# Softplus as one ScalarE function, six front products moved from GpSimd to VectorE, and new step sequences, in an RWKV-7 block

## Chip, cores and metric

The kernel runs on one core of one Trainium2 chip. The metric is device time in microseconds. A core has TensorE (PE), which multiplies matrices, VectorE (DVE), ScalarE (ACT), GpSimd (POOL) and SyncE (SP), which here issues DMAs. Each engine runs its own instructions in order. They are tied together by semaphores alone.

## The reference

For x of shape (2, 4096, 256) the block computes, with a layer norm xn in front:

```
xx  = previous token of xn - xn
mix = tanh((xn + xx*maa_x) @ w1) @ w2                 (four parts)
xrg, xwa, xk, xv = xn + xx * (maa_. + mix_.)
r, k, v = xrg @ wr.T, xk @ wk.T, xv @ wv.T
w   = -softplus(-(time_decay + tanh(xwa @ d1) @ d2)) - 0.5
g   = tanh(xrg @ g1) @ g2
kk  = normalised per head (k + tanh(xk @ kkk1) @ kkk2)
a, ma, mk = sigmoid(aaaaa + xwa@..), sigmoid(misc_a + xwa@..), sigmoid(misc_k + xk@..)
k   = k*ma + k*a*(1-ma);   k = k * exp(min(w*mk, 0))
S_t = S_{t-1}*diag(exp(w_t)) + (S_{t-1} (-kk)) (kk*a)^T + v_t k_t^T ;  y_t = S_t r_t
y   = (group norm(y)*ln_w + ln_b + bonus) * g @ wo.T
out = x + y * silu(ffn(xn))                           (ffn: gated, hidden 768)
```

All of it is float32, with 4 heads of 64 in each of the 2 sequences.

## The kernel before

The 4096 tokens are cut into 16 tiles t of 256 tokens; a tile covers both sequences, so it has 512 columns. In a tile the recurrence is worked in 8 chunks of 32 tokens, each chunk in 4 blocks of 8. A big product over a tile has the shape 128x1024 (two halves of the 256 channels by 512 columns), half of it 128x512.

The program is a software pipeline of sections. In a section, four tiles are in work at once: `norm` of tile i+1, the front of tile i (`mixing`, `decays`, `key`, `receptance`, `value`, `update`, `pairs`), the recurrence `back` and the `ffn` of tile i-1, and `output` of tile i-2. Each of these stages is a Python generator for each engine, and each `yield` ends a step. What comes after what on an engine is written out by hand as a string of letters (`ORDER` for full sections, `FIRST` before there is a recurrence, `LAST` when there is no front): each letter takes the next step of its stream, in `walk`. The letters are L norm, F mixing, D decays, K key, R receptance, V value, E update, X pairs, N ffn, B back, O output.

The steps used below are these.

- On PE: `mixin`, `mix0`, `mix1` (L) make the four mix parts. `lora` and `z` (F) make the decay's logits and those of the sigmoids. `k0`, `k1`, `hk`, `kk`, `rn` (K), `gh`, `r0`, `r1` (R), `v0`, `v1`, `vT0`, `vT1`, `g0`, `g1` (V) are the projections. N steps are half groups of four matmuls of the feed-forward. `half`, `matrix`, `KT` 0 to 3 (X) make pairwise products and transposed keys. `band`, `corner` and, for each chunk c, `state`, `u`, `values`, `s`, `y` are the recurrence (B). `yT0`, `yT1`, `out0`, `out1` are the output.
- On ACT: `na`, `nma` are sigmoids, `z0`, `z1` hold the decay's first activations, `mk0`, `mk1` sigmoids, `sqk` squares for the key's norm, `rn_ln` and `rn` its inverse root by Ln and Exp, `em`, `er`, `ek`, `es`, `EF` exponentials.
- On DVE: `mix..` are the mix products (L989), `nd`, `cs2`, `cs4`, `cs8` and `fl3` to `fl0` the cumulated decay, `unit`, `inv0` to `inv14`, `flip` the inversion of the small triangular matrices, `kk0`, `kk1`, `rn0`, `rn1`, `k`, `b`, `rk`, `dm`, `qa`, `qa0`, `hat0`, `hat1` the front's products, `near`, `far`, `keys` the keys for PE.
- On POOL: the mix sums (L1273), for each chunk the faded state `state` (L1334), and the products `mixa`, `kk`, `mkz`, `kem`, `e3`, `qr`.

The decay is made in four parts. ACT takes Abs and Relu of z + decay (L718, L721). ACT then applies Exp and Ln(1 + .) to the whole tile (L850, L853), which gives softplus as relu(-x) + ln(1 + exp(-|x|)). DVE adds 0.5 (`n`, L999) and limits to 20 (`nd`, L1002).

PSUM is held as two rings. `ring` has four banks, `spare` four others, shared with the recurrence's chunk banks. Each use waits until the use four places before it has been emptied (`room`, `early_room`). `KT3` and the mix matmuls are neighbours in `ring`. The matmul helper `project` (L381) has many callers: `lora` and the projections.

SP issues the DMAs in order (`invert`). The matrices go out to DRAM and come back in another layout. The inverse's part leaves after DVE's `flip`, comes back as `first`, for which SP also waits for `out1` of PE, and only then can PE run `band`.

Of the kernel before, what the change touches and what calls it, by code (L numbers as in the profile page):

```python
# [1525 lines left out]
```

## Time and profile before

| | us |
|---|---|
| median of 3 runs | 1663.23 |
| lowest and highest | 1652.58, 1664.02 |
| profiled execution, its own time | 1652.18 |
| profiled execution, span from first to last instruction | 1650.7 |
| granted TensorE clock, mean (1 is 2.4 GHz) | 0.981 |

The profile is one execution, and its durations add up to its own span and not to the median. Engines overlap: their busy times are shares of the same span. Busy time counts an instruction from its start to its end. TensorE's matmuls overlap each other, so the step from one group's start to the next group's start is the cost of a group. L and a number is a line of the kernel, and a name with an arrow says what is written from what.

### The profile page before, as it was taken

How to read it: one execution, taken by the hardware profiler on the slowest of the kernel's cores; microseconds unless marked ns; L12 is line 12 of the kernel's file. 1: busy time of each engine (PE TensorE's matmuls, PEld its weight loads, DVE VectorE, ACT ScalarE, POOL GpSimd, SP SyncE). 2: the span in 40 equal slices, each digit the busy share in tenths (PEclk: the TensorE clock that was granted, in tenths of full speed). 3: DMA queues.
4: the chain of work that ended last, by engine and by line, in shares of the span. 5: the costliest groups of instructions: out<-in, count | busy, mean ns of one | idle time of the engine just before them, and what ended most of it. 6: DMA issues, size and time to landing. Idle time of an engine off the chain costs nothing.

```text
span 1650.7 us, 48315 instructions
## 1 busy us (share of the span) xinstructions
PE 1543.8 (94%) x20288; PEld 1084.1 (66%) x20288; DVE 1157.5 (70%) x2581; ACT 1126.8 (68%) x1954; POOL 579.1 (35%) x459
## 2 busy tenths in 40 slices
PE   4599999999999999999999999999999999999887
PEld 1266667576676757667676766757667675766665
DVE  3776768778676877867678676767767687686633
ACT  4858586676858767685876858667585876768412
POOL 3424432433433244343423433243343323434101
PEclk9789999999999999999999999999999999999989
DMA  4011110201112021111202111020111202111020
GB/s 145 14 19 34 32 33 16 60 19 32 34 33 46 16 47 31 32 33 26 53 16 42 36 33 33 17 59 19 32 34 27 52 16 47 31 33 33 11 55 27
DMA packets 251431, 57.86 MB, mean 35 GB/s; under 512 B 223696, under 2 KB 250704, under 8 KB 251088
## 3 DMA queue, kind: packets, MB, share of 16 engines
q1 hardware_dynamic: 241936, 41.95, 13.5%
q10 hardware_dynamic: 9280, 12.81, 2.2%
q8 instruction: 162, 2.65, 0.7%
q14 instruction: 53, 0.43, 0.1%
HBM read 36.38 MB, written 18.35 MB: 33 GB/s over the span
## 4 chain that ended last, share of the span: by engine, by line
PE 88%; DVE 4%; ACT 3%; POOL 2%; issue 2%; DMA 1%; SPq 0%; ACTq 0%; DVEq 0%; POOLq 0%
PE bank L535 22%; PE chunk L381 15%; PE bank L545 10%; PE bank L510 8%; PE bank L665 4%; PE chunk L643 3%; PE chunk L615 3%; PE chunk L590 3%; POOL big L1273 2%; PE bank L480 2%; PE chunk L629 2%; PE bank L381 2%; PE bank L486 2%; PE chunk L599 2%; PE bank L518 1%
## 5 line engine op out<-in xcount | busy, mean ns | idle before, releaser
L1334 POOL TENSOR_TENSOR SF<-ST,CT 128x256 f32<-128x256 f32 x128 | 101.9, 796 | 302.1 <-DVE ST L1200 302.1
L535 PE MATMUL bank<-xT,wu 128*128 128x256 f32 x768 | 203.3, 396 | 0.0
L535 PE MATMUL bank<-xT,wg 128*128 128x256 f32 x768 | 198.2, 390 | 0.0
L545 PE MATMUL bank<-wd,hT 128*128 128x256 f32 x768 | 179.5, 388 | 1.9 <-DVE hT L1160 1.9
L535 PEld LDWEIGHTS bank<-xT,wg 128*128 128x128 f32 x768 | 141.5, 191 | 49.6 <-issue 30.3
L545 PEld LDWEIGHTS bank<-wd,hT 128*128 128x128 f32 x768 | 144.1, 193 | 23.3 <-DVE hT L1160 3.0
L535 PEld LDWEIGHTS bank<-xT,wu 128*128 128x128 f32 x768 | 135.4, 189 | 33.0 <-issue 9.9
L381 PE MATMUL chunk<-KS,W 128*128 128x512 f32 x320 | 148.8, 603 | 1.5 <-POOL KS L1273 1.5
L510 PE MATMUL bank<-qpad,KS 128*64 128x32 f32 x4096 | 144.1, 226 | 5.6 <-DVE KE L1132 4.0
L510 PEld LDWEIGHTS bank<-qpad,KS 128*64 128x64 f32 x4096 | 132.0, 141 | 17.4 <-issue 8.7
L381 PE MATMUL chunk<-big,W 128*112 128x512 f32 (+1 forms) x256 | 125.6, 614 | 16.9 <-POOL big L1273 16.9
L912 ACT ACTIVATE rhs<-chunk 96x256 f32<-96x256 f32 x128 | 48.7, 380 | 127.0 <-PE chunk L615 125.7
L895 ACT ACTIVATE Y<-chunk 32x256 f32<-32x256 f32 x256 | 96.3, 376 | 51.2 <-PE chunk L599 47.9
L869 ACT ACTIVATE sg<-bank 128x512 f32<-128x512 f32 x96 | 57.0, 594 | 100.9 <-PE bank L535 94.3
L1283 POOL MEMSET KS<- 128x800 f32 x16 | 12.2, 765 | 291.0 <-PE chunk L381 291.0
L381 PEld LDWEIGHTS chunk<-KS,W 128*128 128x128 f32 x320 | 59.8, 191 | 70.7 <-issue 66.8
L844 ACT ACTIVATE KT<-bank 128x512 f32<-128x512 f32 x64 | 38.2, 597 | 95.4 <-PE bank L518 94.7
L1195 DVE COPY VU<-chunk 32x256 f32<-32x256 f32 x128 | 53.4, 417 | 66.7 <-PE chunk L629 63.5
L1160 DVE TENSOR_TENSOR hT<-sg,bank 128x512 f32<-128x512 f32 x96 | 65.7, 684 | 45.2 <-PE bank L535 33.1
L1273 POOL TENSOR_TENSOR big<-VU,xT 128x512 f32<-128x512 f32 x64 | 74.3, 1197 | 58.2 <-DVE VU L989 58.2
L832 ACT ACTIVATE qpad<-big 64x256 f32<-64x256 f32 x256 | 91.6, 405 | 1.2
L1273 POOL TENSOR_TENSOR KS<-VU,xT 128x512 f32<-128x512 f32 x64 | 91.2, 1459 | 0.0
(161 smaller groups left out, 3484.8 us busy)
## 6 DMA issues: line engine op xcount, KB each, us to landing
smalls<-in_x SPq DMA_DIRECT2D x32, 256.0 KB, 3.1
Y<-in_x SPq DMA_DIRECT2D x32, 256.0 KB, 3.1
out<-fsil ACTq DMA_DIRECT2D x32, 256.0 KB, 2.5
scrA<-AM SPq DMA_DIRECT2D x64, 64.0 KB, 1.9
hat<-scrB SPq DMA_DIRECT2D x32, 128.0 KB, 3.1
hat<-scrF SPq DMA_DIRECT2D x32, 128.0 KB, 3.1
KE<-scrA SPq DMA_DIRECT2D x64, 32.0 KB, 2.2
scrT<-KE SPq DMA_DIRECT2D x16, 128.0 KB, 1.7
```

What stands on the lines that cost most here:

```text
L381: m = pe.matmul(o, weights[:, h, :], x[:, h, :], start=(h == 0), stop=(h == NH - 1))
L510: q = pe.matmul(oc[:, :, BL * j:BL * j + BL], K[:, 2 * n + b, 64 * j:64 * j + 64], Q[:, 2 * n + b, j, :, :, :].rearrange("p a b e -> p (a ...
L535: q = pe.matmul(o[:, TT_ * n2:TT_ * n2 + TT_], w[:, h, 128 * (n + n2):128 * (n + n2) + 128], x_now[:, h], start=(h == 0), stop=(h == NH - 1))
L545: q = pe.matmul(o[:, 256 * m:256 * m + 256], hT[:, n, 128 * m:128 * m + 128], wd[:, n, :], start=(n == 0), stop=(n == NF - 1))
L665: q = pe.matmul(o[:, 256 * n2:256 * n2 + 256], yb[:, h, 128 * m:128 * m + 128], wo[:, h, :], start=(h == 0), stop=(h == NH - 1))
L832: i = act.activation(Q[p0:p0 + 64, :, :, hh, x, :], own[p0:p0 + 64, qs], ACT.Copy)
L869: act.activation(sg[:, :], ring.tile(key)[:, :], ACT.Silu).then_inc(*sg_ready.up)
L895: i = act.activation(by_batch, RY[64 * x + 32:64 * x + 64, :, :].rearrange("p b (g n) -> p b g n", g=NH), ACT.Copy)
L1160: i = dve.tensor_tensor(hT[:, n:n + 2, :], sg[:, :].rearrange("p (n c) -> p n c", n=2), ring.tile(key)[:, :].rearrange("p (n c) -> p n c", ...
L1195: dve.tensor_copy(VU[par][32:64, c, :].rearrange("p (g x n) -> p x g n", g=NH, x=2), PU[32:64, :, :].rearrange("p x (g n) -> p x g n", g=N ...
L1273: pool.tensor_tensor(columns(dst[:, h, :]), columns(w[:, h, :]), x_now_of(par, h), ALU.add).then_inc(*moved.up)
L1334: pool.tensor_tensor(SF[:, :, :, :], ST[:, :, :, :], fade[:, c].unsqueeze(3).to_broadcast([128, B, NH, N]), ALU.mult).then_inc(*faded.up)
```

## The change

It does three things. `Softplus` of ACT takes the place of Abs, Relu, Exp and Ln, and DVE's `n` and `nd` become one instruction. The six POOL products `mixa`, `kk`, `mkz`, `kem`, `e3`, `qr` become DVE instructions of the same shape (scalar_tensor_tensor). All strings of `ORDER` and `FIRST` are new; `LAST` stays.

```diff
-ORDER = {"pe": ("FNNKOOFNNOKNOVNNNKNNVKRRRKBNNBVNNNNBBNBBNBNBNBBVBBEBNVBBNBBVBBBNBBNBXBBXBBNXBNBBXBBXBBBLBBNXBXBBXBBN"
-            "LXXXLLX"),
-         "act": ("NFKFFFFFFDDVKNKNVKKRKEOOBRKBVKRXDXXBVBNNBNBBVVBXBBXBVBBBBBVBNBBLBBXBLLXBBBXBBXNXLX"),
-         "dve": ("OBOOBBBNBBBBBOBBOBBDBDBNDBBDKDDKKDKNEDDXEEBXBNXBXBXEXXXBEXBNXXBXXBLXBBXXXXBLXXBXNBXXXXXBXXXBLLXXXBBX"
-             "XLLLLLLLL"),
-         "pool": ("DBEXEFKXBBBBLLBBBBLLLLLLLL")}
+ORDER = {"pe": ("NNNFNKOOFNNORVNNNNKKOVKRBNKBNRNNVBBNBBNBNBNBBVNNBBEBVBBNBBVBNBBNBBXBXBBNXBBNBNBBXBBXBXBBNBBLBNBBXXBB"
+            "LXXXXLL"),
+         "act": ("NFKFFFFFRFVNKKNVOKKKBEBOKRKRDXXBXBVNBVNBBVVNBBBXBVVBBXBBBBNBBXXBLBBLXLBXBBNBBLXX"),
+         "dve": ("ONBOOBBBBBDBBBBBBBNBBDBBDDOOKKDXEFKKNDEDEXDKEEBXBXXXNBXBXXXBEXXBEXXBXNBXLBXXXBXXBLXBXNXXXBXXXBXLXLBX"
+             "XXBBXXLLLLLLLL"),
+         "pool": ("DBBBBBBLBBLBLLLLLLLL")}
...
-                            act.activation(az[:, g, :], spare.tile(key), ACT.Abs, bias=v("decay", g))
...
-                            act.activation(rz[:, g, :], spare.tile(key), ACT.Relu, bias=nv("decay", g), scale=-1.0).then_inc(*z_ready.up)
+                            act.activation(rz[:, g, :], spare.tile(key), ACT.Softplus, bias=nv("decay", g), scale=-1.0).then_inc(*z_ready.up)
...
-                act.wait_ge(*z_ready(t))
-                act.activation(az[:, :, :], az[:, :, :], ACT.Exp, scale=-1.0).then_inc(*dz_exp.up)
-                yield "exp"
-                act.wait_ge(*dz_exp(t))
-                act.activation(az[:, :, :], az[:, :, :], ACT.Ln, bias=one[:, 0:1]).then_inc(*dz_ln.up)
-                yield "ln"
...
-                dve.wait_ge(*dz_ln(t))
-                dve.scalar_tensor_tensor(out=rz[:, :, :], in0=az[:, :, :], scalar=0.5, in1=rz[:, :, :], op0=ALU.add, op1=ALU.add).then_inc(*n_ready.up)
-                yield "n"
-                dve.wait_ge(*n_ready(t))
-                dve.tensor_scalar(nd[:, :, :], rz[:, :, :], MAXDECAY, None, ALU.min).then_inc(*nd_ready.up)
+                dve.wait_ge(*z_ready(t))
+                dve.tensor_scalar(nd[:, :, :], rz[:, :, :], 0.5, MAXDECAY, ALU.add, ALU.min).then_inc(*nd_ready.up)
...
+                dve.wait_ge(*rn_ready(t))
+                dve.scalar_tensor_tensor(out=kk[:, :, :], in0=kk[:, :, :], scalar=1.0, in1=rn[:, :, :], op0=ALU.mult, op1=ALU.mult).then_inc(*kk_ready.up)
+                yield "kk"
...
-                pool.wait_ge(*rn_ready(t))
-                pool.tensor_tensor(kk[:, :, :], kk[:, :, :], rn[:, :, :], ALU.mult).then_inc(*kk_ready.up)
-                yield "kk"
...
```

The other five products change engine in the same way as `kk`. On PE the end of a full section was

```
... y7 ffn1 mixin KT2 half3 matrix3 mix0 mix1 KT3 | lora gate00 gate01 k0 yT0 yT1 z up00 up01 out0 k1 ... kk gh r0 r1 rn band
```

and is now

```
... y7 mixin KT2 half3 matrix3 KT3 mix0 mix1 | gate00 gate01 up00 lora up01 k0 yT0 yT1 z gate02 gate03 out0 gh v0 up02 up03 gate04 gate05 k1 hk out1 v1 kk r0 band up04 rn corner up05 r1
```

On DVE the front of a full section is now: groupnorm, up00, unit, yT0, yT1, inv0 to inv4, nd, inv5 to inv11, up02, inv12, inv13, cs2, inv14, flip, cs4, cs8, out0, out1, kk0, kk1, fl3, e3, mkz, mixa, rn0, rn1, up04, fl2, kem, fl1, k, dm, fl0, kk, b, rk, u0, qa, s0, qa0, qr, hat0. On ACT it is: gate00, lora, k0, na0, nma0, z0, z1, na1, gh, nma1, v0, gate02, k1, hk, gate04, v1, out0, mk0, mk1, sqk, band, em, corner, out1, rn_ln, r0, rn, r1, EF, er, ek, state0, es, u0, vT00, ffn0, state1.

## Rows read from the trace of the kernel before

**Rows 1.** The page, part 1: busy us, share of the span, instructions.
```profile
PE 1543.8 (94%) x20288; PEld 1084.1 (66%) x20288; DVE 1157.5 (70%) x2581; ACT 1126.8 (68%) x1954; POOL 579.1 (35%) x459
```

**Rows 2.** Windows: length, busy per engine, then granted PE clock, DMA share, GB/s.
```profile
0.00:34.40 34.40, 11.62 (x36) 4.77 (x36) 12.93 (x27) 10.93 (x14) 12.33 (x21) 1.00 0.49 174
34.40:109.60 75.20, 51.97 (x404) 30.66 (x404) 54.94 (x98) 51.28 (x80) 30.66 (x21) 0.80 0.06 13
301.20:398.50 97.30, 94.56 (x1272) 66.86 (x1272) 71.89 (x162) 70.21 (x123) 36.01 (x29) 1.00 0.17 34
985.00:1084.00 99.00, 96.25 (x1268) 67.44 (x1269) 70.89 (x161) 70.03 (x123) 36.00 (x28) 0.98 0.16 33
1475.70:1650.70 175.00, 154.68 (x2112) 115.28 (x2112) 91.43 (x212) 82.38 (x154) 33.55 (x28) 0.94 0.15 33
976.00:980.00 4.00, 3.63 (x6) 1.73 (x7) 3.50 (x5) 0.01 (x1) 4.00 (x5) 0.62 0.45 45
805.00:826.00 21.00, 21.00 (x145) 13.90 (x144) 8.12 (x16) 18.33 (x25) 12.61 (x7) 1.00 0.34 64
```

**Rows 3.** Waits of PE: who waited for whom, us in total, times, longest.
```profile
PE chunk L381 <- POOL big L1273: 16.9, 16, 2.6
...
PE bank L518 <- DVE VU L989: 12.1, 14, 0.9
PE bank L495 <- DVE KS L1057: 9.5, 1, 9.5
...
PE chunk L421 <- issue: 5.4, 13, 0.5
...
PE bank L510 <- DVE KE L1132: 4.0, 1, 4.0
```

**Rows 4.** Timeline of PE: start, length, instruction, count, idle before it and releaser.
```profile
679.13 1.14 PE L402 MATMUL chunk<-smalls,W 32*128 32x512 f32 x8
...
682.13 0.66 PE L518 MATMUL bank<-con,KE 128*128 128x128 f32 x4 [0.87 <-DVE VU L989]
683.77 1.94 PE L381 MATMUL chunk<-big,W 128*112 128x512 f32 x4 [0.98 <-POOL big L1273]
...
690.42 0.70 PE L421 MATMUL chunk<-smalls,W 32*128 32x512 f32 x2 [0.39 <-issue]
```

**Rows 5.** Timeline of PE, the same place three periods on.
```profile
976.37 3.18 PE L381 MATMUL chunk<-big,W 128*112 128x512 f32 x4 [0.99 <-POOL big L1273]
```

**Rows 6.** Groups by line and form, ACT: busy us, mean ns, idle before.
```profile
L718 ACT ACTIVATE big<-chunk,vec 128x512 f32<-128x512 f32 x32 | 22.0, 689 | 0.0
...
L850 ACT ACT_TABLE_LOAD x16 | 20.5, 1283 | 0.3
...
L853 ACT ACTIVATE big<-big,one 128x1024 f32<-128x1024 f32 x16 | 18.4, 1149 | 0.2
...
L850 ACT ACTIVATE big<-big 128x1024 f32<-128x1024 f32 x16 | 16.9, 1057 | 0.2
```

**Rows 7.** Groups by line and form, POOL.
```profile
L1278 POOL TENSOR_TENSOR big<-KB,big 128x1024 f32<-128x1024 f32 x16 | 38.1, 2380 | 1.5 <-ACT big L712 1.5
```

**Rows 8.** Groups by line and form, DVE.
```profile
L1227 DVE SCALAR_TENSOR_TENSOR hat<-hat,vec,gT 128x512 f32<-128x512 f32 x32 | 32.3, 1010 | 1.1
...
L1049 DVE SCALAR_TENSOR_TENSOR KB<-KB,KS 128x1024 f32<-128x1024 f32 x16 | 19.6, 1225 | 36.6 <-POOL KS L1288 36.6
...
L1055 DVE SCALAR_TENSOR_TENSOR KS<-KS,vec,KB 128x512 f32<-128x512 f32 x16 | 11.9, 746 | 0.7 <-issue 0.7
```

**Rows 9.** The page, part 6: a DMA, KB, us from issue to landing.
```profile
hat<-scrF SPq DMA_DIRECT2D x32, 128.0 KB, 3.1
```

**Rows 10.** Timeline of ACT: sqk, first half and second half.
```profile
811.44 0.63 ACT L745 ACTIVATE KS<-KS 128x512 f32<-128x512 f32 x1 [0.22 <-DVE KS L1027]
812.09 1.28 ACT L747 ACTIVATE KS<-KS 64x512 f32<-64x512 f32 x2
```

**Rows 11.** Timeline of PE between the end of kk and rn.
```profile
808.52 5.42 PE L381 MATMUL chunk<-KS,W 128*128 128x512 f32 x12
```

More of the change, by code:

```diff
@@ L135, in program @@
         mask = sb("mask", [128, 64], U32)
-        one = sb("one", [128, 2])
-        minus_half = one[:, 1:2]
+        minus_half = sb("minus_half", [128, 1])[:, 0:1]
         wg = sb("wg", [128, NH, DH])
@@ L993, in mixing @@
             def mixing(t):
-                yield from ()
+                dve.wait_ge(*nma_ready(t))
+                dve.scalar_tensor_tensor(out=mix_a[:, :, :], in0=na[:, :, :], scalar=1.0, in1=nma[:, :, :], op0=ALU.mult, op1=ALU.mult).then_inc(*mixa_ready.up)
+                yield "mixa"
             def decays(t):
                 rz = gT[t % 2]
-                dve.wait_ge(*dz_ln(t))
-                dve.scalar_tensor_tensor(out=rz[:, :, :], in0=az[:, :, :], scalar=0.5, in1=rz[:, :, :], op0=ALU.add, op1=ALU.add).then_inc(*n_ready.up)
-                yield "n"
-                dve.wait_ge(*n_ready(t))
-                dve.tensor_scalar(nd[:, :, :], rz[:, :, :], MAXDECAY, None, ALU.min).then_inc(*nd_ready.up)
+                dve.wait_ge(*z_ready(t))
+                dve.tensor_scalar(nd[:, :, :], rz[:, :, :], 0.5, MAXDECAY, ALU.add, ALU.min).then_inc(*nd_ready.up)
                 yield "nd"
@@ L1042, in update @@
                 par = t % 2
+                rz = gT[t % 2]
+                dve.wait_ge(*z_ready(t))
+                dve.wait_ge(*mk_ready(t))
+                dve.scalar_tensor_tensor(out=mk[:, :, :], in0=rz[:, :, :], scalar=0.5, in1=mk[:, :, :], op0=ALU.add, op1=ALU.mult).then_inc(*mkz_ready.up)
+                yield "mkz"
+                dve.wait_ge(*em_ready(t))
+                dve.wait_ge(*kk_raw(t))
+                dve.scalar_tensor_tensor(out=kT[:, :, :], in0=kT[:, :, :], scalar=1.0, in1=mk[:, :, :], op0=ALU.mult, op1=ALU.mult).then_inc(*kem_ready.up)
+                yield "kem"
                 dve.wait_ge(*mixa_ready(t))
@@ L1070, in pairs @@
                 dve.wait_ge(*cs_ready(t))
+                dve.wait_ge(*mixed(t))
+                dve.scalar_tensor_tensor(out=e3b, in0=csb[:, :, BL - 1:BL].to_broadcast([128, G8, BL]), scalar=1.0, in1=csb,
+                                         op0=ALU.mult, op1=ALU.subtract).then_inc(*e3_raw.up)
+                yield "e3"
                 dve.wait_ge(*kem_ready(t))
@@ L1082, in pairs @@
                 yield "qa0"
+                dve.wait_ge(*qa_most(t))
+                dve.wait_ge(*r_ready(t))
+                dve.scalar_tensor_tensor(out=qr[:, :, :], in0=er[:, :, :], scalar=1.0, in1=rT[:, :, :], op0=ALU.mult, op1=ALU.mult).then_inc(*qr_ready.up)
+                yield "qr"
                 dve.wait_ge(*qr_ready(t))
@@ L1276, in mixing @@
             def mixing(t):
-                pool.wait_ge(*nma_ready(t))
-                pool.tensor_tensor(mix_a[:, :, :], na[:, :, :], nma[:, :, :], ALU.mult).then_inc(*mixa_ready.up)
-                yield "mixa"
+                yield from ()
             def decays(t):
@@ L1286, in key @@
             def key(t):
-                pool.wait_ge(*rn_ready(t))
-                pool.tensor_tensor(kk[:, :, :], kk[:, :, :], rn[:, :, :], ALU.mult).then_inc(*kk_ready.up)
-                yield "kk"
+                yield from ()
             def receptance(t):
@@ L1297, in update @@
             def update(t):
[L1298 to L1317 removed]
+                yield from ()
+            def pairs(t):
+                yield from ()
             def ffn(t):
@@ L1344, in output @@
                 yield from ()
-            for level, col in ((1.0, 0), (-0.5, 1)):
-                pool.memset(one[:, col:col + 1], level).then_inc(s_clear, 1)
+            pool.memset(minus_half, -0.5).then_inc(s_clear, 1)
             for z in (xT2[1][:, :, :, TT_:TT_ + 1], ST[:, :, :, :], TT[:, :, :], qpad[0][:, :, :, :, :, :], qpad[1][:, :, :, :, :, :]):
```

34 lines of the change are left out of this document (8 added, 26 removed).

## Prediction

> **What bounds the kernel now.** I read the page first, its busy times by engine. TensorE (PE) is busy 1543.8 of the span's 1650.7 us [rows 1]. The diff touches none of its 20288 matmuls, so only the 107 us in which PE has no work can shrink, plus what a lower clock costs. The busy times by stretch show where they are [rows 2]: a steady period has 2.7 us without work in 97.3, the first front 23.2 in 75.2, the loads and first `norm` before it 22.8, and the tail from the last `z` 20.3 in 175, mostly in an order that the diff leaves alone. PE's waits name them [rows 3]. The timeline of one section boundary places them [rows 4]: `KT3` (L518) stands behind `mix1` and waits 0.87 us for a bank that VectorE's (DVE's) mix product L989 frees. `lora` (L381) then waits 0.98 us for the second mix sum of GpSimd (POOL, L1273), and `z` (L421) loses 0.39 us.
>
> The granted clock matters too. Periods of 99.0 us instead of 97.3 hold a stretch at 1.2 instead of 2.4 GHz [rows 2]. The clock falls right behind the KT3 and lora waits: the same four `lora` matmuls take 3.18 us instead of 1.94 [rows 4, 5]. The profiled execution has three such periods (the `lora` at about 976, 1075 and 1175 us), each 1.7 us longer.
>
> **The change, part by part.** I call the start of `mix0` on PE 0 and walk the new order with durations of before. From one group's start to the next is less than its printed length: an N half (L535, four matmuls) 0.87, a 128x512 projection (L381) 1.72 to 1.78 us, as the timeline's starts show.
>
> *The boundary.* The new PE order is matrix3, KT3, mix0, mix1, gate00, gate01, up00, lora, up01, k0, yT0, yT1, z. `KT3` is now ahead of the mix matmuls and needs nothing of L989: -0.87. Behind `mix1` (over at 2.0) come three N halves, so `lora` is reached at 4.6. Before, POOL's second sum let it start at 683.77 - 679.13 = 4.64 [rows 4], and on that way nothing changes, so of the 0.98 about 0.05 stays. `z` keeps its 0.4 (10.5 to 12.75).
>
> *Softplus.* Out per section: two Abs (0.69), Exp (1.06), Ln (1.15) and their two table loads (1.28) [rows 6]. Relu becomes Softplus. No row shows Softplus; its neighbours of this shape take 0.69, which I take, with 0.57 (their spacing) and 1.4 (Abs and Relu together) as bounds. Nor does a row show whether Softplus shares a table with Sigmoid. If it does, no load comes in; if not, one before `z0` and one before `na1` do. I take not, since here Exp and Ln too, common as they are, have a load each. ScalarE (ACT) then runs load, na0, nma0 (to 13.0), load, z0, z1 (15.6), load, na1, gh (18.6), nma1 (19.2). PE's `gh` at 16.2 needs z0 (15.0), `v0` at 17.9 needs z1: hidden. At 1.4 us each, `up02` on DVE and the inversion behind it slip by 1.4, and with a band load that has 0.7 to spare that is up to 10 us in all.
>
> By the row a table load is 1.28 us with at most 0.3 around it [rows 6]. The Trainium skill ("ScalarE: Activation LUTs", What ACT_TABLE_LOAD costs) budgets about 2.66 us for each switch, a drain included, and its section on table sets asks to batch by set, which a Softplus among Sigmoids does not. By its figure two loads out and two in cancel as well.
>
> *Products on DVE.* A POOL product of 128x1024 takes 2.38 us [rows 7], five of the six moved are like it; on DVE the shape takes 1.22 [rows 8]. DVE gains six and loses `n`: +6.1 a section, 98 us in all, to about 1255. POOL falls to about 360. The cover is DVE's own waiting: between 805 and 826 us it is busy 8.1 of 21 us [rows 2], part of the rest in waits for these very POOL products.
>
> Side by side the two engines may hinder each other: DVE's L1227 takes 1.01 us on mean, L1055 of the same shape 0.75 [rows 8], and L1227 runs while POOL's mix sums do. The Trainium skill ("SBUF — State Buffer", Who interferes with whom) says that a DVE instruction with two SBUF inputs contends with a GpSimd one that reads SBUF, which all six products are. The trace agrees so far. By that rule a state product (L1334) could stand behind one of them, 1.2 us. PE's next state update is further off than that, so I add nothing.
>
> *The front.* After `z` PE has gate02, gate03, out0 (from 14.5; its input is ready at 14.0 to 14.6: 0.1 lost), gh, v0, four N halves, k1, hk, out1, v1 (to 29.95), kk, r0, band, up04, and wants `rn` at 34.8. `rn` needs `sqk` from ACT, and ACT starts its part when v1 ends: v1 0.6, load 1.28, mk0 and mk1 1.26, sqk 1.93 [rows 6, 10] give 35.2. That is a **new wait of 0.5 us**; before, three projections (5.4 us) lay between kk and rn [rows 11]. DVE: inversion to 25.1, cs4, cs8, out0, out1, kk0, kk1 (32.5), fl3, e3, mkz (35.5), mixa, rn0, rn1 (37.9), up04, fl2, kem (40.3), k, dm (42.9), kk (behind ACT's rn, 43.7), b, rk (48.4), u0 (48.85). PE wants `s0` at 49.4: **0.5 us to spare**, and ACT's u0 (48.85, behind er, ek, es) has as much. PE's `u1` waits 0.15 for ACT's `state1`. From `half0` on DVE is 0.5 us or more ahead at each step. The band's load left SP 2.5 us after the flip by the timeline of SP and takes 3.1 us [rows 9]; now it also stands behind out1, and lands by 32.1. PE wants it at 32.8.
>
> Per period: -0.87 - 0.93 + 0.5 + 0.15 + 0.1 + 0.05 = -1.0, in 14 periods **-14 us**. The three clock falls behind the waits removed: 3 x 1.7 = **-5 us**.
>
> *First front and tail.* There PE waits in plain sequence, 9.5 us for rk and 4.0 for the keys besides others [rows 3]. `nd` can start about 5 us earlier, kk is 1.15 shorter; against it, ACT takes k0 ahead of lora (+1), and the next x and the vT copies stay. I get the first `half0` at 76 to 77 us instead of 80.6 and 3 to 4 us of this at the second `z`, which also has two N halves more behind it (1.7 us less in the tail): **-5 us**, bounds 0 and -12 (the 13.5 us of the two waits less what must stay).
>
> Sum: 1652.2 (the profiled execution's own time) - 14 - 5 - 5 = 1628. That execution lies 11 us under the median of before, 1663.2. Six more clock falls at the same boundary would explain it, but no row shows the other runs. With the boundary closed I expect the median near the profiled one and add 2: **1630 us**, 2% less.
>
> **The rivals.**
> - *New waits take the place* (0.20). rn, s0 and the band stand within 0.7 us of their data in my walk. If they lose 1.0 us a period more, the boundary's gain is given back: 1628 + 14 = 1642, with the clock falls back as well 1647, with the median's distance 1658. For it: ACT has no pause up to sqk. Against: inside a steady section PE had no wait longer than 0.4 us. This is most of "same".
> - *DVE becomes the bound of the front* (0.09), the slower side. Place: rk, then u0 on DVE, `s0` on PE. DVE has 7.3 us of products more ahead of u0. Each us beyond the 0.5 to spare costs 14; slower by over 1% needs a wait of 3.6 us a period at `s0`, a DVE that is 4.1 us later than in my walk. At 4.8 late it gives about 1690. Against: 12.9 us idle before in this stretch, 7.3 to place.
> - *Softplus shares Sigmoid's table and rn does not wait* (0.10). Two loads (2.57 us) less let gate02 and the inversion run ahead, and without the 0.5 and other small waits it is 1628 - 7 - 4 = 1617.
> - *Only the head gains; the boundary waits move but stay* (0.05): 1652 - 5 = 1647 profiled, median 1655 to 1658.
> - Forecast: 0.56.
>
> **How the numbers follow.** About 1%, 16.6 us, is what measurement tells from no change: faster is below 1646.6, slower above 1679.9. Faster: 0.56 + 0.10 + 0.04 of the first rival = 0.70. Slower: 0.09, with 0.01 for Softplus at 1.4 and a late band together = 0.10. Same: 0.20. The range goes from 1610, the third rival with a better head, to 1658, the top of the first and fourth; outside lie the slower rival and 0.1 of others. The likeliest case's own range is 1618 to 1643.
>
> **What would show each step.** PE's wait at the chunk L381 for POOL L1273 falls from 16.9 us to under 5, and L518's for L989 is gone; else the boundary is wrong. The period from L421 to L421 is 96.2 to 96.5; at 97 or more the first rival holds, and the line that waits names the step (L455 for ACT: sqk; L564 for DMA: band; L643 for DVE: the slower rival). Softplus rows are 0.69 us, table loads stay nine a section. DVE is busy about 1255 us, POOL 360. The first L510 starts at 76 to 77 us. No clock fall at the boundary in the steady part. The prediction falls if the products take clearly over 1.22 us on DVE, or if PE's own busy time grows.

## The result, and the profile after

| | before | after |
|---|---|---|
| median, us | 1663.62 (4 runs, 1652.58 to 1664.95) | 1605.62 (4 runs, 1604.55 to 1612.88) |
| ratio after to before | | 0.9675, 95% interval 0.9632 to 0.9717 |
| profiled execution, its own time | 1652.18 | 1604.90 |
| its span | 1650.7 | 1603.4 |
| granted TensorE clock, mean | 0.981 | 0.988 |

The change makes the kernel 58 us faster, 3.3%. The forecast was 1630, with a range from 1610 to 1658. The direction was right, but the time lies 4.4 us below the range, and the gain is 58 us where 33 were forecast. L numbers of after are its own lines, mostly one or two below those of before.

First the page of after, part 1, beside [rows 1]:

```profile
PE 1520.5 (95%) x20288; PEld 1064.9 (66%) x20288; DVE 1243.6 (78%) x2661; ACT 1069.5 (67%) x1889; POOL 354.6 (22%) x362
```

PE has the same 20288 matmuls and is busy 23 us less. The forecast had only the clock falls' 5 us of that. DVE (1255 forecast) and POOL (360) came out near what was worked out.

The windows of after, cut as [rows 2] (length, busy per engine, granted clock, DMA share, GB/s): first front, a steady period, tail.

```profile
35.50:103.60 68.10, 50.43 (x414) 30.84 (x415) 55.60 (x106) 46.67 (x75) 13.64 (x13) 0.82 0.10 19
386.70:481.80 95.10, 93.76 (x1268) 65.82 (x1268) 77.52 (x167) 66.60 (x119) 22.05 (x23) 1.00 0.17 34
1434.70:1603.40 168.70, 148.19 (x2104) 110.16 (x2104) 97.06 (x216) 79.02 (x150) 19.45 (x22) 0.96 0.16 34
```

A steady period, from `z` to `z`, takes 95.12 us. Before, an undisturbed one took 97.26. That splits into 1.39 us less idle (2.75 to 1.36) and 0.75 less busy (94.51 to 93.76). The first front is 7.1 us shorter, the tail 6.3.

PE's waits in after, beside [rows 3] (engine, line, releaser, us in total, times, longest):

```profile
PE bank L534 <- DVE VU L981: 13.5, 15, 1.0
PE bank L494 <- DVE KS L1060: 7.8, 1, 7.8
...
PE chunk L420 <- issue: 5.5, 14, 0.4
PE bank L509 <- DVE KE L1143: 4.0, 1, 4.0
...
PE chunk L380 <- POOL big L1284: 2.9, 2, 2.6
```

The wait of `lora` (L380) for POOL fell from 16.9 to 2.9 us. KT3's wait for the mix product is gone, but `gate00` (L534) now waits for the same product, 13.5 us in 15 waits. PE's timeline at the boundary shows it, beside [rows 4]:

```profile
469.94 0.66 PE L517 MATMUL bank<-con,KE 128*128 128x128 f32 x4
470.52 1.14 PE L401 MATMUL chunk<-smalls,W 32*128 32x512 f32 x8
471.49 1.04 PE L406 MATMUL bank<-smalls,W 32*128 32x512 f32 x8
473.42 2.00 PE L534 MATMUL bank<-xT,wg 128*128 128x256 f32 x8 [0.89 <-DVE VU L981]
475.25 1.03 PE L534 MATMUL bank<-xT,wu 128*128 128x256 f32 x4
476.12 1.88 PE L380 MATMUL chunk<-big,W 128*112 128x512 f32 x4
```

The ring is filled in turn. Whatever follows the four mix matmuls of the second half takes a bank that DVE has to empty first. Before, that was `KT3`; now it is `gate00`.

The operations themselves, from the groups by line and form of ACT and then of DVE (count, busy us, mean ns, idle before):

```profile
L719 ACT ACT_TABLE_LOAD x16 | 20.5, 1283 | 12.0 <-DVE hat L1238 11.9
...
L719 ACT ACTIVATE gT<-chunk,nvec 128x512 f32<-128x512 f32 x32 | 20.3, 684 | 0.2
```

```profile
L1092 DVE SCALAR_TENSOR_TENSOR big<-big,KS 128x1024 f32<-128x1024 f32 x16 | 26.0, 1625 | 0.0
...
L987 DVE SCALAR_TENSOR_TENSOR big<-KB,big 128x1024 f32<-128x1024 f32 x16 | 19.5, 1217 | 0.0
```

Softplus takes 0.68 us and has a table load of its own. Five of the six products take 1.22 us on DVE. `qr` (L1092) takes 1.63 on mean. It begins while POOL works on a state product (L1325), on POOL's and DVE's timelines:

```profile
426.85 0.71 POOL L1325 TENSOR_TENSOR SF<-ST,CT 128x256 f32<-128x256 f32 x1 [18.99 <-DVE ST L1211]
426.99 1.65 DVE L1092 SCALAR_TENSOR_TENSOR big<-big,KS 128x1024 f32<-128x1024 f32 x1
```

It ends 1.08 us after the state product, which is nearly its whole length of 1.22. The experiments come back to this.

### The profile page after: what moved, and what is told of

It is laid out like the page before. It is cut to its first block, busy times and chain, and to the rows that moved or that the text cites. A ratio compares the mean times of both kernels' runs of the same rounds, so it can differ in the third digit from the quotient of the medians.

```text
span 1603.4 us, 48245 instructions
## 1 busy us (share of the span) xinstructions
PE 1520.5 (95%) x20288; PEld 1064.9 (66%) x20288; DVE 1243.6 (78%) x2661; ACT 1069.5 (67%) x1889; POOL 354.6 (22%) x362
## 4 chain that ended last, share of the span: by engine, by line
PE 92%; DVE 3%; ACT 2%; issue 1%; POOL 0%; DMA 0%; SPq 0%; ACTq 0%; DVEq 0%; POOLq 0%
PE bank L534 23%; PE chunk L380 15%; PE bank L544 11%; PE bank L509 8%; PE bank L664 4%; PE chunk L642 3%; PE chunk L614 3%; PE chunk L589 3%; PE chunk L598 2%; PE bank L485 2%; PE bank L380 2%; PE bank L517 2%; PE bank L479 2%; PE chunk L628 2%; DVE VU L981 1%
## 5 line engine op out<-in xcount | busy, mean ns | idle before, releaser
L1325 POOL TENSOR_TENSOR SF<-ST,CT 128x256 f32<-128x256 f32 x128 | 99.7, 779 | 728.8 <-DVE ST L1211 728.8
L534 PE MATMUL bank<-xT,wg 128*128 128x256 f32 x768 | 197.2, 391 | 14.2 <-DVE VU L981 13.5
L534 PE MATMUL bank<-xT,wu 128*128 128x256 f32 x768 | 207.3, 395 | 0.0
L534 PEld LDWEIGHTS bank<-xT,wg 128*128 128x128 f32 x768 | 136.3, 189 | 57.6 <-DVE VU L981 24.1
L534 PEld LDWEIGHTS bank<-xT,wu 128*128 128x128 f32 x768 | 135.1, 188 | 34.8 <-issue 14.5
L380 PE MATMUL chunk<-KS,W 128*128 128x512 f32 x320 | 149.6, 598 | 0.3 <-ACT gT L719 0.3
L380 PE MATMUL chunk<-big,W 128*112 128x512 f32 (+1 forms) x256 | 117.9, 593 | 5.1 <-POOL big L1284 2.9
L380 PEld LDWEIGHTS chunk<-KS,W 128*128 128x128 f32 x320 | 59.2, 189 | 62.9 <-issue 48.5
L1211 DVE TENSOR_TENSOR ST<-SF,chunk 128x256 f32<-128x256 f32 x128 | 53.8, 420 | 37.2 <-PE chunk L642 34.4
L380 PEld LDWEIGHTS chunk<-big,W 128*112 128x112 f32 (+1 forms) x256 | 46.5, 182 | 49.7 <-issue 39.4
```

Of the source, the lines that this page charges most:

```text
L380: m = pe.matmul(o, weights[:, h, :], x[:, h, :], start=(h == 0), stop=(h == NH - 1))
L534: q = pe.matmul(o[:, TT_ * n2:TT_ * n2 + TT_], w[:, h, 128 * (n + n2):128 * (n + n2) + 128], x_now[:, h], start=(h == 0), stop=(h == NH - 1))
L1211: dve.tensor_tensor(ST[:, :, :, :].rearrange("p b h n -> p b (h n)"), SF[:, :, :, :].rearrange("p b h n -> p b (h n)"), PS, ALU.add).then_ ...
L1325: pool.tensor_tensor(SF[:, :, :, :], ST[:, :, :, :], fade[:, c].unsqueeze(3).to_broadcast([128, B, NH, N]), ALU.mult).then_inc(*faded.up)
```

## The experiments

Each kernel ran on one chip with runs of before beside it. "Period" is the time from one `z` to the next, worked out from the starts of the `z` matmuls in the trace. There are 13 full ones in each kernel behind the first. I give the shortest and how many of the 13 are longer than it by over 1.2 us. In all kernels of the tables below these are periods with more time at half clock than the shortest one. The start of the program, up to the first `z`, took between 34.3 and 39.3 us in these traces, whatever the kernel. A single profile is therefore a poor measure of the total and a good one of the period.

### Which part of the change carries the gain

S is Softplus, D the six products on DVE, O the new orders. The first four kernels are S, D, S with D, and O, each on before:

```diff
 S (e1)
-act.activation(az[:, g, :], spare.tile(key), ACT.Abs, bias=v("decay", g))
-act.activation(rz[:, g, :], spare.tile(key), ACT.Relu, bias=nv("decay", g), scale=-1.0)
+act.activation(rz[:, g, :], spare.tile(key), ACT.Softplus, bias=nv("decay", g), scale=-1.0)
-dve.scalar_tensor_tensor(out=rz[:, :, :], in0=az[:, :, :], scalar=0.5, in1=rz[:, :, :], op0=ALU.add, op1=ALU.add)
+dve.tensor_scalar(rz[:, :, :], rz[:, :, :], 0.5, None, ALU.add)
 D (e2)
-pool: zero state0 mkz e3 kem mixa kk qr state1
+pool: zero state0 state1
-dve: kk1 rn0 fl2 rn1 ... fl0 dm b rk ... qa0 u1 hat0
+dve: kk1 mkz e3 mixa rn0 fl2 rn1 kem ... fl0 dm kk b rk ... qa0 qr u1 hat0
```

e1 also leaves out Exp, Ln and their letters. e4 is both edits. O (e9) has the new ORDER and FIRST, with exp, ln, n and the six POOL products put back in.

> Softplus alone: the old orders without the letters of Exp and Ln, POOL's six products stay, DVE's n only adds 0.5. Theory A (the gain is in the new orders on PE, the operations only make room): ACT loses 2.9 us a section and PE's busy time stays at 1544 +- 2; the steady periods stay within 0.2 us of 97.3, at most 2 us off in the first front. Time 0.995 to 1.003 of before. Rival B (the operations themselves shorten the periods, since ACT and DVE come earlier to what PE waits for): 0.7 us or more a period, 10 us or more in all, 0.994 or less.

> Six products on DVE alone, put into the old DVE order by hand; the four ACT functions and PE's order stay. Theory A (the orders hold the gain): PE's waits at lora for POOL's mix sum and at KT3 for DVE's mix product stay at about 1.0 and 0.9 us a period, since they hang on the mix products and sums and on none of the six; the first front gains some 2 to 4 us because kk takes 1.2 instead of 2.4 us and POOL's queue is short; 0.995 to 1.003 of before. Rival B: POOL, 36% instead of 60% busy in the front, gives the mix sums earlier, lora's wait is under 0.3 us a period and 10 us or more go: 0.994 or less. Rival C: DVE's 7 us more make PE wait in the front: over 1.005.

> Softplus and the six products on DVE together, in the old orders (the change without its new sequences on PE). Theory A: the first front gives 3 to 5 us, the periods nothing: 0.994 to 1.001 of before, so over 40 of the 47 us hang on the new orders. Rival B (the operations are the gain): 0.985 or less.

> The new orders alone: Abs, Relu, Exp, Ln, n and nd stay, and so do the six products on POOL; the steps that the new strings lack are put where their data allow. Theory A (PE's new order is the gain, wherever the products run, as long as they come in time): the interleaving of the u and y matmuls and the removed waits bring periods of 95.1 to 95.7; 0.97 to 0.98 of before. Rival D (the new PE order needs the room that the operations make): POOL's products come 1 to 2 us late each, PE waits for kk, rn or s0 in each period, periods of 97 or more: 0.99 or more.

Then after without D and after without S:

```diff
 O, S (e7)
-pool: zero state0 state1
+pool: zero mkz e3 kem mixa kk state0 qr state1
 O, D (e10)
-act: gh nma1 v0
+act: gh nma1 exp ln v0
-dve: inv4 nd inv5 ... inv11 up02 inv12 inv13
+dve: inv4 inv5 ... inv11 n up02 inv12 nd inv13
```

> After, with the six products back on POOL and Softplus kept. The new orders with all the old operations measured 1.06 of before, after 0.9675. Theory A1 (the products on DVE are the room that the new orders need): still 1.04 to 1.06 of before. Theory A2 (Softplus is the room): 0.97 to 0.985. If both carry a share, between.

> After, with the four ACT functions and DVE's n back, the products on DVE. Theory A1 (the products on DVE are the room): 0.97 to 0.985 of before. Theory A2 (Softplus is it: nd comes only behind the inversion now, so decay, cs, fl3 and the products hang on Ln): 1.03 to 1.06. Between if both.

| kernel | ratio to before, 95% | shortest period | longer, of 13 | first front |
|---|---|---|---|---|
| before | 1 | 97.26 | 3 | 75.2 |
| S | 1.0027 (0.9995 to 1.0059) | 97.7 | 12 | 76.0 |
| D | 1.0002 (0.9966 to 1.0038) | 97.3 | 8 | 75.5 |
| S, D | 1.0036 (1.0005 to 1.0068) | 97.7 | 11 | 75.8 |
| O | 1.0595 (1.0566 to 1.0623) | 102.75 | 8 | 88.7 |
| O, S | 1.0238 (1.0162 to 1.0313) | 99.9 | 7 | 85.6 |
| O, D | 1.0174 (1.0101 to 1.0247) | 99.8 | 7 | 73.7 |
| O, S, D (after) | 0.9675 (0.9632 to 0.9717) | 95.12 | 0 | 68.1 |

The operations alone are worth nothing, and the orders alone cost 6%. The whole gain lies in the combination. For S, D and both, theory A held for the time. The first front gained nothing, though, and with S the shortest periods are 0.4 us longer instead of within 0.2: PE has a new wait there, 0.2 us for ACT's `na1`, in front of which a table load now stands. For O rival D held, and more strongly than it said. In the two kernels with O and one of S and D even the shortest periods have a mean clock of 0.98, so part of their loss is the clock's.

The traces name what goes wrong without D. PE's waits in the kernel with O and S:

```profile
PE chunk L626 <- ACT rhs L902: 48.7, 16, 3.3
```

`u0` waits 3.3 us in each period for ACT, and ACT waits 4.19 us for DVE's `fl` steps ahead of its own `EF`. ACT's timeline, and then DVE's, show why:

```profile
458.38 0.87 ACT L848 ACTIVATE EF<-KS 128x800 f32<-128x800 f32 x1 [4.19 <-DVE KS L1004]
```

```profile
449.27 3.99 DVE L1004 TENSOR_TENSOR KS<-KS,big 128x64 f32<-128x64 f32 x2
453.11 1.22 DVE L1033 SCALAR_TENSOR_TENSOR KB<-big,KB 128x1024 f32<-128x1024 f32 x1
454.25 3.37 DVE L1060 SCALAR_TENSOR_TENSOR big<-big 128x1024 f32<-128x1024 f32 x1
```

and POOL's:

```profile
448.40 2.36 POOL L1293 TENSOR_TENSOR KB<-KB,big 128x1024 f32<-128x1024 f32 x1 [0.38 <-ACT big L798]
450.72 2.35 POOL L1266 TENSOR_TENSOR big<-KB,big 128x1024 f32<-128x1024 f32 x1
453.79 2.75 POOL L1276 TENSOR_TENSOR KS<-KS 128x1024 f32<-128x1024 f32 x1 [0.71 <-ACT KS L749]
```

`dm` (L1060) is one product that takes 1.22 us elsewhere. Here it begins while POOL works on `kk`, takes 3.37 us, and ends 1.1 us after POOL's product ends (457.62 against 456.54). The small `fl` steps take 2.2 us (a mean of 2219 ns for the 128x96 form, 326 in after). DVE has no idle time between 449.27 and 461.6, so it waits for no result of POOL there: the lost time lies in its own operations. An operation that reads two SBUF operands on DVE seems to stand still until POOL's is over, as `qr` did in after. POOL pays as well: `kk` (L1276), which starts while DVE works on L1033, takes 2.75 us, and the products before it 2.36. The Trainium skill ("SBUF — State Buffer", Who interferes with whom) says that a DVE instruction with two SBUF inputs contends with a GpSimd instruction that reads SBUF. The trace agrees, with 3.37 us for 1.22. That the one that comes second is held up for all of the other's instruction, the page says of DVE's two-port modes. Here the times fit it for these operations too, since `dm` ends 1.08 us behind POOL's end.

Without S, DVE's timeline in the kernel with O and D:

```profile
425.74 1.23 DVE L999 SCALAR_TENSOR_TENSOR gT<-big,gT 128x1024 f32<-128x1024 f32 x1 [4.74 <-ACT big L851]
...
432.56 0.68 DVE L1255 TENSOR_TENSOR fsil<-fsil,bank 128x512 f32<-128x512 f32 x1
```

and what it means for PE's `kk`, which needs the banks of `out0` and `out1`:

```profile
434.71 2.09 PE L445 MATMUL bank<-smalls,W 16*128 16x512 f32 x8 [2.84 <-DVE fsil L1255]
```

The new DVE order has the decay in the middle of the inversion. In this kernel `n` stands behind `inv11` and waits 4.7 us for ACT's Ln. Everything behind it (`flip`, `out0`, `out1`) is late, until PE waits 2.84 us. In e9 both waits stand side by side (39.9 us at L445, 36.6 at L627). The places of `n`, `nd` and the POOL letters were my choice, so 1.02 and 1.06 hold for these placements and not for the best ones.

### The section boundary on PE

Four kernels make a table: KT3 ahead of the mix matmuls (new) or behind (old), and `lora` behind `gate00 gate01 up00` (new) or ahead (old). Each is after with PE's order changed and nothing else.

```diff
 after
 ... matrix3 KT3 mix0 mix1 | gate00 gate01 up00 lora up01 ...
 e5
+... matrix3 mix0 mix1 KT3 | lora gate00 gate01 up00 up01 ...
 e15
+... matrix3 mix0 mix1 KT3 | gate00 gate01 up00 lora up01 ...
 e16
+... matrix3 KT3 mix0 mix1 | lora gate00 gate01 up00 up01 ...
```

> After with the old section boundary on PE: KT3 behind mix0 and mix1 again, lora ahead of gate00 and gate01; all else as after. Prediction's step: the boundary is worth 0.87 + 0.93 us a period, 15 periods, 27 us with nothing given back: 1630 +- 5. Rival: of KT3's 0.87 us nothing had gone, since gate00 waits 0.9 us in its place; then only lora's 0.93 us comes back, 14 us, and 1620 +- 4. If clock falls return behind the two waits, up to 5 us more.

> After with KT3 alone put back behind mix0 and mix1; lora stays behind gate00, gate01, up00. In before with lora moved, KT3 waited 0.86 and gate00 0.66 us for mix products. Theory (moving KT3 ahead turned two waits into one): the same two waits here, 1.5 instead of 0.9 us, periods 95.7, 9 us more than after: 1614 +- 3, without clock falls. Rival (the prediction's step, KT3's wait goes as a whole): 0.87 us a period, 13 us: 1619 +- 3.

> After with lora alone put back ahead of gate00 and gate01; KT3 stays ahead of mix0. Lora may start when POOL's second mix sum is there, 4.64 us behind mix0's start, and PE then waits 2.6 us in one piece, against 0.9 at gate00 in after: 1.7 us a period more, 96.8 to 96.9, 25 us: 1631. Theory on the clock (a fall follows a longer wait of PE at this place, one of 2.6 us more surely than 0.9 and 1.1 close together): periods of 98.5 in most of the 14, up to 24 us more, 1631 to 1655. Rival (the falls come from something else than this wait): at most 3 of 14 such periods.

| KT3, lora | kernel | median | ratio, 95% | shortest period | waits in it | longer, of 13 |
|---|---|---|---|---|---|---|
| old, old | e5 | 1636.81 | 0.9856 (0.9772 to 0.9939) | 96.30 | KT3 0.86, lora 1.07 | 6 |
| old, new | e15 | 1623.68 | 0.9779 (0.9744 to 0.9813) | 95.95 | KT3 0.86, gate00 0.66 | 0 |
| new, old | e16 | 1655.59 | 0.9963 (0.9924 to 1.0002) | 96.81 | lora 2.64 | 10 |
| new, new | after | 1605.62 | 0.9675 (0.9632 to 0.9717) | 95.12 | gate00 0.89 | 0 |

The two moves do not add up. Moving KT3 is worth 0.83 us when `lora` has moved and costs 0.51 when it has not. Moving `lora` is worth 0.35 with KT3 behind and 1.69 with it ahead. Together they are worth 1.18 us of undisturbed period. The prediction had 0.87 + 0.93 = 1.80. For e15 my theory said 95.7 and the rival 96.0: the rival's size was right for the period, since not only the waits differ (1.52 against 0.89) but also PE's busy time by 0.2 us. The time of e5 (1636.81) lies in the range of the prediction's step with clock falls, but by another sum: 1.18 us a period, and seven falls in its 14 periods, 12 us where I had allowed 5. The time of e15 (1623.68) lies above both ranges. In its profile the 14 periods give 11.9 of the 17.9 us to after, and the start and the first front nearly all of the rest.

The clock weighs nearly as much as the waits. Windows of e16, two neighbouring periods of the same work and the same 3.1 us idle:

```profile
299.40:396.20 96.80, 93.72 (x1268) 65.84 (x1268) 76.69 (x167) 66.59 (x119) 22.05 (x22) 1.00 0.17 34
396.20:494.80 98.60, 95.47 (x1272) 66.52 (x1272) 76.51 (x167) 66.70 (x119) 21.99 (x22) 0.98 0.16 33
```

and the `lora` behind such a fall in e5, a timeline row of PE, at half the speed of the row of after (1.88):

```profile
481.48 3.45 PE L378 MATMUL chunk<-big,W 128*112 128x512 f32 x4 [1.07 <-POOL big L1282]
```

The theory of the e16 expectation held: 10 of 13 periods have the fall, 1.7 us each. Without a wait at `lora`, no period has one at the boundary (after, e15, and e12 below), although e15 has 1.52 us of waits at the same place. The waits alone do not set how often it comes: before, D, S with D, and S all wait 0.87 us at KT3 and 0.98 to 1.09 at `lora`, and have 3, 8, 11 and 12 falls.

The same move made on before, `lora` alone:

```diff
 e12
-... mix0 mix1 KT3 | lora gate00 gate01 k0 ...
+... mix0 mix1 KT3 | gate00 gate01 lora k0 ...
```

> Before, with lora moved behind gate00 and gate01 on PE alone. The 0.99 us wait of lora for the mix sum goes, KT3's 0.87 us stays. Theory A: 1.0 us a period less, 14 us, and if the clock falls hang on both waits standing within 3 us of each other, these go too, 1.7 us in each of the 3 to 13 periods that have them: 0.976 to 0.987 of before. Rival: the falls stay, since KT3's wait stays: 0.990 to 0.993. Second rival: z, k0 and the sigmoids behind lora are late by the 2 us of the two gate steps and PE waits at z: 0.998 or more.

It measured 1640.47 us, 0.9870 (0.9820 to 0.9921). The period fell from 97.26 to 97.0 only, because `gate00` waits 0.66 us where `lora` had waited 0.99. But none of the 13 periods has a clock fall, against 3, 8, 11 and 12 of 13 in the four kernels above with the old PE order. So about four of its 16 to 18 us are the wait, and the larger part is the clock. The granted clocks of the runs say the same: the median is 0.985 for e12 and 0.978 for before beside it, and 0.007 of 1650 us is 12 us. That is an estimate, which takes it that PE sets the pace. Theory A had the total right, at the edge of its range, and the wait too large.

### Work between state and y, u

PE's `y` and `u` of a chunk both follow `state`. In two chunks before has nothing between them, and it shows in PE's timeline of before:

```profile
355.49 0.46 PE L615 MATMUL chunk<-ST,hat 64*64 64x64 f32 x16
355.88 0.46 PE L599 MATMUL chunk<-VU,AM 32*64 32x64 f32 x16
356.45 0.46 PE L629 MATMUL chunk<-rhs,TT 32*64 32x64 f32 x16
356.84 1.13 PE L535 MATMUL bank<-xT,wg 128*128 128x256 f32 x4
```

and with a gate step between, in after:

```profile
427.28 0.46 PE L614 MATMUL chunk<-ST,hat 64*64 64x64 f32 x16
427.67 1.13 PE L534 MATMUL bank<-xT,wu 128*128 128x256 f32 x4
428.73 0.28 PE L598 MATMUL chunk<-VU,AM 32*64 32x64 f32 x4
428.78 0.28 PE L628 MATMUL chunk<-rhs,TT 32*64 32x64 f32 x4
428.84 0.24 PE L598 MATMUL chunk<-VU,AM 32*64 32x64 f32 x4
...
429.17 1.16 PE L479 MATMUL bank<-con,bv 128*128 128x128 f32 x8
```

In the first the pair takes 0.96 us, from 355.88 to 356.84: `u` has to wait for ACT's copy of `state` (L912, which ends at 356.40), and `y` has run alone by then. In the second the data of both are there, their matmuls run in turns, and the 32 of them take 0.44. After has a step there in every chunk. e6 takes it out again in two of them, e11 puts it into before:

```diff
 e6, on after
-... state3 up13 y2 u3 ...   ... state6 KT1 y5 u6 ...
+... state3 y2 u3 up13 ...   ... state6 y5 u6 KT1 ...
 e11, on before
-... state3 y2 u3 gate14 ... s5 matrix1 state6 y5 u6 ...
+... state3 gate14 y2 u3 ... s5 state6 matrix1 y5 u6 ...
```

> After with the steps of other work taken out from between state and y, u in two of the chunks (3 and 6), put right behind u; nothing else moves. Theory F (u and y run interleaved only if PE has other work between state and them; without it y takes 0.57 and u 0.39 us one behind the other, and ACT's part of u is waited for): 0.55 us a chunk more, 1.1 a period, 16 to 18 us in all: 1622 +- 4. Rival (PE's busy time fell for another reason, and the work is only moved): within 3 us of after.

> Before, with a step of other work put between state and y, u in the two chunks (3 and 6) where its order has none: gate14 ahead of y2, matrix1 ahead of y5. All operations stay as before, products on POOL. In the after kernel taking such steps out cost 0.62 us a period. Theory F: the same comes back here, with the 0.11 us waits of u for ACT, 0.3 to 0.4 us a chunk: periods 0.6 to 0.8 us shorter, 8 to 12 us, 0.993 to 0.995 of before, if the clock falls stay as often. Rival: the chain u, s, state on VectorE, which has less cover then, takes it back: 0.998 or more.

e6 measured 1617.61 us, 12 more than after, 0.9727 (0.9658 to 0.9796). Its period is 95.74, 0.62 more, nearly all periods alike: 0.42 busy and two waits of 0.11. That is 8.7 us in 14 periods; in the profiled execution the start and the first front took 6 us more as well. Theory F holds in kind. The size is little over half of what it said, since a step that follows `u` directly costs less than one between: the two halves that now stand together behind `u3` take 1.92 us, and 1.06 each in after.

e11 shows the other side: 1669.69 us, 1.0065 (1.0027 to 1.0104), and 3 of 13 periods with a fall. PE's busy time falls by the same 0.6 us a period, 94.56 to 93.95, and yet the period grows to 98.54:

```profile
507.70:606.30 98.60, 93.95 (x1271) 66.25 (x1272) 71.17 (x162) 70.21 (x123) 34.85 (x28) 1.00 0.16 33
```

PE's timeline of e11 has three waits that the same place of before does not have:

```profile
663.36 0.46 PE L588 MATMUL chunk<-VU,AM 32*64 32x64 f32 x16 [0.83 <-ACT Y L893]
...
675.06 0.46 PE L613 MATMUL chunk<-ST,hat 64*64 64x64 f32 x16 [0.73 <-DVE ST L1198]
...
678.97 0.46 PE L641 MATMUL chunk<-VU,KT 64*64 64x64 f32 x16 [0.54 <-ACT VU L916]
```

The step that went between state and u is missing where it stood, as cover for ACT's and DVE's copies, and their own orders were not changed with it. The rival held in the time; the copies of ACT take part beside DVE's chain, which it named. e13 joins both edits on before:

```diff
 e13
 e11, and lora behind gate00 gate01 as in e12
```

> The edits of the last two in one kernel: before, with lora behind gate01 and a step between state and y, u in chunks 3 and 6. Nothing but PE's order differs from before: four ACT functions and six POOL products stay. If these are the two sources of the gain in the periods, and each is free of the new operations, clean periods are 95.5 to 95.8 and the time 1617 to 1628, 0.972 to 0.98 of before. If the operations' room is needed for them, 0.985 or more.

It measured 1661.94 us, 1.0022 (0.9982 to 1.0063), with a period of 98.26. That is the case of 0.985 or more, in which the edits need the room of the operations. Compared with e12 (96.99) the fillers cost 1.27 us a period here too. PE's order alone, so changed, does not bring the gain.

### The wait that is left

gate00's 0.89 us hangs on the mix product that frees its bank. e8 lets the first halves use the ring and the second halves the spare banks, so that the ring's banks are freed earlier. e14 also lets each mix matmul wait for its own bank only:

```diff
 e8
-four = [early_room(t, (t, "mix0", n), mixed(t, 2 * n + 1)) for n in range(4)]
+four = [room((t, "mix", n), mixed(t, 2 * n + 1)) for n in range(4)]
...
-four = [room((t, "mix", n), mixed(t, 2 * n + 2)) for n in range(4)]
+four = [early_room(t, (t, "mix1", n), mixed(t, 2 * n + 2)) for n in range(4)]
 e14, beside that, for both halves
-four = [room((t, "mix", n), mixed(t, 2 * n + 1)) for n in range(4)]
-for n, o in enumerate(four):
+for n in range(4):
+    o = room((t, "mix", n), mixed(t, 2 * n + 1))
```

> After, with the two halves of each mix part swapped between the two rings of banks: the first half's matmuls write the banks that gate00 takes next, so VectorE frees them four products earlier. Theory (gate00's 0.89 us a period is a wait for the mix product that frees its bank, and nothing else waits behind it): that wait is gone, 15 times, 13 us less than after: 1592 +- 4, periods of 94.2. Rival: another use of the spare banks, z or lora, waits for the second half's products instead, or lora for the mix sum, and the time stays at 1602 to 1608.

> The swap of banks of e8, and the four mix matmuls of a half now take their banks one at a time, each just ahead of its matmul, instead of all four before the first. In e8 the wait had moved from gate00 to mix0: 0.78 us for ACT's copy of KT3, whose bank only the last of the four needs. Theory: three matmuls run during that wait, 0.3 to 0.6 us a period less, periods 94.5 to 94.8, 1597 to 1602. Rival: what bounds the boundary is the sequence mix0, DVE's mix products, gate00 and lora, and the time stays at 1604 to 1608.

e8 measured 1606.78 us, 0.9669 (0.9614 to 0.9723), with the same period as after, 95.12. gate00's wait is gone and another stands ahead of it, in PE's timeline of e8:

```profile
469.56 0.66 PE L517 MATMUL bank<-con,KE 128*128 128x128 f32 x4
470.99 1.14 PE L401 MATMUL bank<-smalls,W 32*128 32x512 f32 x8 [0.78 <-ACT KT L842]
471.93 1.06 PE L407 MATMUL chunk<-smalls,W 32*128 32x512 f32 x8
473.02 2.00 PE L534 MATMUL bank<-xT,wg 128*128 128x256 f32 x8
```

The last of the four mix matmuls takes the bank of KT3, which ran right before it. Neither side of the expectation named this wait; the time is that of the rival. e14, the same place:

```profile
472.70 1.45 PE L401 MATMUL bank<-smalls,W 32*128 32x512 f32 x7
473.66 0.90 PE L407 MATMUL chunk<-smalls,W 32*128 32x512 f32 x3
473.99 0.59 PE L401 MATMUL bank<-smalls,W 32*128 32x512 f32 x1
...
475.36 2.00 PE L534 MATMUL bank<-xT,wg 128*128 128x256 f32 x8
```

No wait is printed any more, but the last of mix0's eight matmuls starts 1.29 us behind the first (472.70 to 473.99), and those of mix1 stretch around it. From `mix0` to `gate00` it is 2.66 us, against 2.90 in after. The shortest period is 94.87, all 13 within 0.2 of it, and the time 1605.12 us, 0.9658 (0.9633 to 0.9683). By the period it is 0.24 us and by 14 of them 3.4 us better than after; by the times the two can't be told apart. The rival's time came out, and the theory's mechanism with half its size.

## Why the prediction was right or wrong

The differences of the two profiled executions are 47.3 us: 6.0 up to the second `z`, 34.9 in the 14 periods, 6.3 in the tail. The forecast had 24 for the same: some 3.3, 14 + 5, and 1.7. The other 11 of the 58 are the distance of before's profile to its median. They were in the forecast too, less 2 us.

So 16 of the 23 us that are missing lie in the undisturbed periods: 2.14 us each where the sum had 1.0. That 1.14 is made up of 0.8 of new waits that did not come, 0.62 of busy time that was not in the sum, 0.22 of another wait, and 0.12 unplaced, less the 0.62 by which the boundary was put too high. The boundary's excess and the missing busy time, 0.62 each, cancel in the number, and that is luck.

- **"Only the 107 us in which PE has no work can shrink."** This step failed. PE's busy time depends on the order, as y and u show: in a period without clock falls it went from 94.51 to 93.76 us. e6 measured 0.62 us a period for the steps between `state` and `y`, `u` (0.42 busy, 0.2 waits), 9 us in all, and nothing of it was in my sum. Of the 23 us that PE is busy less in all, some 10 are these 0.75 a period; most of the others are the clock. The rows for it were in the trace of before: chunks with a step between and chunks without lie side by side.
- **The boundary, -1.80 a period.** -1.18 undisturbed. KT3 was sized right (0.83 against 0.87), but only together with `lora`, and its wait went to `gate00`. I took each step's own wait away and did not ask which bank the next user of the ring needs. My walk had `lora` start 4.6 us behind mix0; it starts 5.6 behind it (470.52 to 476.12).
- **New small waits, +0.8.** None came, and with 11 us in 14 periods this is the term that moved the number most. `rn`, `s0`, `u1` and `out0` wait for nothing in the steady periods. Counted from `z`, `sqk` on ACT ended at 24.8 us (24.7 forecast), but PE reached `rn` at 24.9 and not at 24.3: its small steps took some tenths more than I had, which is all it took for ACT to be ready.
- **What the forecast did not name.** The wait of `s7` (0.22 us a period, "PE chunk L643 <- issue: 3.7 us, 16 times" before) is gone. With it the parts are 1.18 + 0.62 + 0.22 = 2.02 of the 2.14 measured. The remaining 0.12 I can't place.
- **The clock, -5.** The place and the price of a fall (1.7 us) were right: the three periods of before's profile account for 5.1 of the 34.9 us, and after has none. The weight was too low. D, S with D, and S have the fall in 8 to 12 of 13 periods, and before's profile in 3. Its granted clock was 0.981. Beside the experiments before's runs have 0.963 to 0.984, with medians of 0.975 to 0.978, so it was one of the luckier executions. e12 shows that the falls alone are worth up to 1% of the time. The 11 us to the median, "six more clock falls", fit that, but no trace of those runs was taken. The runs of after have a median clock of 0.989. By these medians 0.011 to 0.014 of the time, some 20 of the 58 us, are the clock, an estimate again.
- **First front and second `z`.** The forecast's -5 for head and tail has 3 to 4 here. It was -6.0: the start took 1.0 longer and the front 7.1 less. Kernels with the same front have 67.9 to 70.5 us, so between 5 and 7 hold. The first half0 came at 73.7, not 76 to 77. All three parts are needed: with old orders the front is no shorter (75.8), with POOL's products it takes 85.6, with Exp and Ln 73.7.
- **The tail.** -6.3 instead of -1.7, and most of it is not the change. The order of the last section is the same in both. S with D, with the old orders throughout, and D have this:

```profile
1492.10:1660.40 168.30, 148.72 (x2112) 110.98 (x2112) 95.89 (x217) 79.13 (x150) 18.70 (x21) 0.98 0.16 34
1486.90:1672.60 185.70, 167.34 (x2112) 124.25 (x2112) 97.67 (x218) 82.36 (x154) 19.79 (x22) 0.85 0.14 31
```

  The same stretch takes 17 us longer at a mean clock of 0.85 than at 0.98. Before has 0.94 there, and after 0.96. If PE sets the pace, the clock costs before 10.5 us and after 6.7, an estimate from the length and the clock. That leaves some 2 us for the change, near the 1.7 of the forecast. All kernels on the base of after except those with S or D taken out have 168.8 to 169.2. Why the clock falls less in that stretch stays open.
- **Costs of the operations.** Softplus 0.68 with its own table, five products 1.22, nine table loads a section: as forecast. Only `qr` takes 1.65 beside POOL's state product. That kk is 1.15 us shorter and nd earlier did not matter by itself: with the old orders both are there and bring nothing. What mattered for the new orders, and stands nowhere in my sum, is that POOL's products hold up DVE: 3.37 instead of 1.22 us for `dm`. I had looked at L1227's 1.01 us (it is 1.50 beside a mix sum and 0.75 without), found the hint, and added nothing, since I asked only what DVE does to POOL's state products.
- **The rivals.** The slower one did not come. Its mechanism, a DVE that is late for PE, is what happens as soon as the products stay on POOL (e7, at `u0`) or Ln stays in front of `nd` (e10, at `kk`). It was a rival to the orders without the operations. "New waits take the place" came in part, and at a step that it did not name: gate00's wait is 0.89 us, and of the boundary's gain 0.62 was given back where the rival had 1.0.

## What to carry to other kernels

Walk the banks and not only the data: when a step is moved away from a wait on a ring, the next user of the ring inherits the wait, and the worth of one move depends on the others, so test them as a table. Work that needs no new data, put between a producer and two consumers, lets the consumers' matmuls run in turns, but it pays only if the engines that copy for them are reordered too. An operation that shows no gain where it is put in alone may still be what makes a better order possible, and an execution with fewer clock falls than the median is no fair base for what a change can win.
